# Two attention blocks merged on one core: values of merged sequences in bf16 high and low parts, and several small steps moved

## What is computed

```python
# block b: causal self-attention with 8 bit activations and ternary weights
q, k, v = bitlinear(x, Wq), bitlinear(x, Wk), bitlinear(x, Wv)   # 16 query heads, 4 key heads of 32
p = softmax(where(causal, -inf, rope(q) @ rope(k).T * scale))
x = layernorm(x + bitlinear(p @ v, Wo))
# block c: attention to 128 memory tokens, with a mask, a norm and a gate
n = rmsnorm(x, norm_w)
p = softmax(where(mask, (n @ wq.T) @ (ctx @ wk.T).T * scale, -inf))
x = layernorm(x + sigmoid(n @ wg.T) * ((p @ (ctx @ wv.T)) @ wo.T))
```

## Time and profile before

| | |
|---|---|
| Time, median of 3 runs | 3141.37 us (3140.55 to 3145.01) |
| The profiled execution's own time | 3140.32 us |
| Its span, from first to last instruction | 3138.5 us |
| PE busy over the span | 2855.3 us (91%) |
| DVE busy | 1852.7 us (59%) |
| ACT busy | 1584.2 us (50%) |
| POOL busy | 1214.4 us (39%) |
| Mean granted PE clock | 0.963 of full speed |

### The profile page before, as it was taken

One profiled execution on the slowest core, in us unless ns is written; L12 is line 12 of the kernel. 1 busy time (PEld: TensorE's weight loads), 2 busy tenths in 40 slices (PEclk: granted clock), 3 DMA queues, 4 the chain that ended last, 5 costly groups with the idle time before them and its releaser, 6 DMA issues. The chain is left out here.

```text
span 3138.5 us, 49654 instructions
## 1 busy us (share of the span) xinstructions
PE 2855.3 (91%) x17186; PEld 1677.1 (53%) x17186; DVE 1852.7 (59%) x3475; ACT 1584.2 (50%) x3632; POOL 1214.4 (39%) x1234
## 2 busy tenths in 40 slices
PE   6789887999999999689858999999679999999998
PEld 4676753555555555334336777766434444444443
DVE  5788977887787887587466666655522222222224
ACT  7999965655555555454157667665322122212211
POOL 4888967654454543144332111111411222122211
PEclk8999998999999999899969999999789999999999
DMA  4111113000000000310020000000100000000001
GB/s 157 51 44 45 45 45 104 28 8 4 7 7 4 7 4 1 124 38 1 15 103 18 15 14 17 15 18 15 64 1 31 31 32 1 31 32 31 1 1 54
DMA packets 35086, 99.01 MB, mean 32 GB/s; under 512 B 4933, under 2 KB 9413, under 8 KB 31686
## 3 DMA queue, kind: packets, MB, share of 16 engines
q1 hardware_dynamic: 34886, 96.46, 9.1%
HBM read 87.79 MB, written 4.46 MB: 29 GB/s over the span
## 5 line engine op out<-in xcount | busy, mean ns | idle before, releaser
L720 POOL TENSOR_TENSOR m_aTl<-m_prod,m_aTh 128x512 bf16<-128x512 f32 x96 | 111.1, 1157 | 675.4 <-ACT m_aTh L778 675.4
L945 DVE TENSOR_TENSOR m_prod<-m_bank,m_gated 128x512 f32<-128x512 f32 x96 | 66.4, 692 | 507.9 <-ACT m_gated L776 507.9
L1926 POOL TENSOR_TENSOR s_state<-s_state,s_ct 128x512 f32<-128x512 f32 x256 | 326.7, 1300 | 80.6 <-DVE s_state L2101 78.2
L2101 DVE TENSOR_TENSOR_SCAN s_state<-s_decay,s_psd 128x512 f32<-128x512 f32 x256 | 301.9, 1209 | 66.0 <-PE s_psd L2246 32.6
L776 ACT ACTIVATE m_gated<-m_bank 128x512 f32<-128x512 f32 x96 | 57.2, 596 | 550.2 <-PE m_bank L1037 550.2
L1035 PE MATMUL m_bank<-m_xTh,m_wh 128*128 128x512 bf16 x768 | 292.1, 380 | 0.0
L1036 PE MATMUL m_bank<-m_xTl,m_wh 128*128 128x512 bf16 x768 | 292.1, 380 | 0.0
L1037 PE MATMUL m_bank<-m_xTh,m_wl 128*128 128x512 bf16 x768 | 292.1, 380 | 0.0
L2246 PE MATMUL s_psd<-ident,s_v 128*128 128x128 f32 x1024 | 164.2, 285 | 42.8 <-DVE s_state L2101 22.3
L2002 ACT ACTIVATE s_decay<-s_dt,s_nega 128x508 f32<-128x508 f32 x256 | 181.8, 711 | 19.0 <-DVE s_state L2101 18.9
L2015 ACT ACTIVATE s_v<-s_uT,s_bT 128x512 f32<-128x512 f32 x256 | 182.3, 713 | 0.2
(11 more groups left out here) (491 smaller groups left out, 8029.0 us busy)
## 6 DMA issues: line engine op xcount, KB each, us to landing
m_stage<-in_moe_w_dram SPq DMA_DIRECT2D x8, 2352.0 KB, 9.4
s_ct<-ssm_bc SPq DMA_DIRECT2D x64, 256.0 KB, 3.1
X<-in_x_dram SPq DMA_DIRECT2D x4, 1024.0 KB, 11.1
a_cf<-in_ctxT_dram SPq DMA_DIRECT2D x16, 256.0 KB, 2.6
a_wstage<-in_xa_wq_dram SPq DMA_DIRECT2D x8, 512.0 KB, 3.9
a_wstage<-in_xa_wo_dram SPq DMA_DIRECT2D x8, 512.0 KB, 3.9
f_wstage<-in_ffn_wg_dram SPq DMA_DIRECT2D x4, 1024.0 KB, 7.2
f_wstage<-in_ffn_wu_dram SPq DMA_DIRECT2D x4, 1024.0 KB, 6.7
```

Source lines behind the costliest of these rows:

```text
L1926: pool.tensor_tensor(h, h, ct[t % 4][:, s * P:(s + 1) * P].unsqueeze(1).broadcast_to([P, KB, P]), ALU.mult).then_inc(weighted, 1)
L2101: dve.tensor_tensor_scan(state[i % RING][:, :], decay[t % 2][:, s, :, :].rearrange("p m t -> p (m t)"), ps_d[i % 2][:, :], 0.0, ALU.mult, ...
```

## The change

- For sequences that do not run alone, probabilities and values are kept as a bf16 high part and a bf16 low part, in the two halves of the old 32 bit tiles. ACT's copy writes the high part (high_part, to pTh); a new DVE step low_part subtracts it from b_pst and writes the low part (pTl). values then issues three products for each head where there was one. DVE also makes low parts of b's values (128 columns) and of c's values (512 columns), one of each in a turn. Sequences that run alone keep 32 bits.
- The wait that stood on the copy (copied) stands on the low part (low). So the other block's transposes wait for ACT's copy and for DVE's subtraction.
- turn_x moves on PE from the end of the steps of group 2 to group 3, behind turn_output, and from bank 0 to bank 2; copy_x on ACT follows; qx.scalar moves from group 1 to group 2, where it stands behind c's exponentials as before.
- c's memory values go through bank 0 in place of bank 2, so PE waits for mk_low (c_kT) before it computes them.
- On DVE: c's divide from group 0 to group 1, behind b's maxima; keys_low from group 1 to group 2; statistics of c's norm from group 3 to group 1, and its end from group 1 to group 2; qx.clip from 1 to 2; b_sc and b_osc are made earlier.

```diff
@@ class PairCore
+        self.vh = [v[:, :].bitcast(BF16)[:, 0:key_groups * P] for v in self.v]
+        self.vl = [v[:, :].bitcast(BF16)[:, key_groups * P:2 * key_groups * P] for v in self.v]
...
@@ def turn_probs(self, pe, s, g, other, turned_by_other):
-            pe.wait_ge(self.copied.sem, self.copied.at(s, g) if g else self.copied.at(s - 1))
+            pe.wait_ge(self.low.sem, self.low.at(s, g) if g else self.low.at(s - 1))
         if not isinstance(turned_by_other, int) or turned_by_other:
-            pe.wait_ge(other.copied.sem, turned_by_other)
+            pe.wait_ge(other.low.sem, turned_by_other)
...
@@ def values(self, pe, s, g, p):
-            mm = pe.matmul(out, self.pT[:, h, :], self.v[p][:, v:v + self.HW], start=True, stop=True)
+            if self.alone(s):
+                mm = pe.matmul(out, self.pT[:, h * P:(h + 1) * P], self.v[p][:, v:v + self.HW], start=True, stop=True)
+            else:
+                mm = three(pe, out, (self.pTh[:, h, :], self.pTl[:, h, :]),
+                           (self.vh[p][:, v:v + self.HW], self.vl[p][:, v:v + self.HW]), True, True)
         mm.then_inc(self.pv.sem, 1)
...
+    def low_part(self, dve, s, g):
+        if self.alone(s):
+            return
+        dve.wait_ge(self.high.sem, self.high.at(s, g + 1))
+        dve.tensor_tensor(self.pTl.rearrange("p h t -> p (h t)"), self.ps_t[:, :],
+                          self.pTh.rearrange("p h t -> p (h t)"), ALU.subtract).then_inc(self.low.sem, 1)
...
@@ scalar (ACT), turn
-                    if g == 1 and live(s + 2):
-                        qx.scalar(act, s + 2)
                     if g == 2:
+                        if live(s + 2):
+                            qx.scalar(act, s + 2)
...
@@ vector (DVE), new steps
+            def values(k, j):
+                if core.alone(k):
+                    return
+                dve.wait_ge(v_high.sem, v_high.at(k))
+                dve.scalar_tensor_tensor(core.vl[j], bank[2][:, NK:2 * NK], sc[j][:, 2:3], core.vh[j],
+                                         ALU.mult, ALU.subtract).then_inc(core.v_ready.sem, 1)
...
+            def memory_values(n, j):
+                if mcore.alone(n):
+                    return
+                dve.wait_ge(mv_high.sem, mv_high.at(n))
+                dve.scalar_tensor_tensor(mcore.vl[j], bank[0][:, :], mv[j][:, 0:1], mcore.vh[j],
+                                         ALU.mult, ALU.subtract).then_inc(mcore.v_ready.sem, 1)
...
@@ vector (DVE), turn
                     if g == 1:
-                        if live(m + 1):
-                            keys_low(m + 1)
+                        if live(m - 1):
+                            mcore.divide(dve, m - 1, o)
                         if live(s - 1):
                             output(s - 1)
-                        if live(s + 2):
-                            qx.clip(dve, s + 2)
                     if g == 2:
                         if live(s - 1):
                             qo.clip(dve, s - 1)
+                            output_scale(s - 1)
+                        if live(m + 1):
+                            keys_low(m + 1)
...
+                    if live(s):
+                        core.low_part(dve, s, g)
...
+                    if g == 2 and live(s + 2):
+                        qx.clip(dve, s + 2)
...
+                    if live(m):
+                        mcore.low_part(dve, m, g)
                     if g == 0:
                         if live(s - 1):
                             core.divide(dve, s - 1, o)
-                        if live(m - 1):
-                            mcore.divide(dve, m - 1, o)
...
+                    if g == 1 and live(m - 2):
+                        mln.statistics(dve, m - 2)
+                    if g == 2 and live(m - 2):
+                        mln.vector_end(dve, m - 2)
...
@@ tensor (PE)
             def turn_x(n):
                 pe.wait_ge(qx.steps.sem, qx.steps.at(n))
-                wait_of(pe, mk_low, n - LAG - 1)
-                edge(ln.steps, n - 4, 1)
-                out = bank[0][:, 0:256].bitcast(BF16)
+                wait_of(pe, core.k_ready, n - 1)
+                out = bank[2][:, 0:256].bitcast(BF16)
...
             def memory_values(n, j):
-                wait_of(pe, core.k_ready, n + LAG)
-                edge(mcore.q_ready, n)
+                pe.wait_ge(mk_low.sem, mk_low.at(n))
                 weights_split(n, 4)
-                product(bank[2][:, :], (cTh[j], cTl[j]), weights["v"], mproj)
+                product(bank[0][:, :], (cTh[j], cTl[j]), weights["v"], mproj)
...
-                    if g == 2:
-                        if live(s + 1):
-                            turn_query(s + 1)
-                            turn_key(s + 1)
+                    if g == 2 and live(s + 1):
+                        turn_query(s + 1)
+                        turn_key(s + 1)
+                    if g == 3:
+                        if live(s - 1):
+                            turn_output(s - 1)
                         if live(s + 2):
                             turn_x(s + 2)
-                    if g == 3 and live(s - 1):
-                        turn_output(s - 1)
```

More of the change, by code:

```diff
@@ L2402, in __init__ @@
         self.turned = Count(fr, f"{tag}_turned", 4)
-        self.copied = Count(fr, f"{tag}_copied", 4)
+        self.high = Count(fr, f"{tag}_high", 4)
+        self.low = Count(fr, f"{tag}_low", 4)
         self.pv = Count(fr, f"{tag}_pv", 4)
@@ L2445, in values @@
     def values(self, pe, s, g, p):
-        pe.wait_ge(self.copied.sem, self.copied.at(s, g + 1))
+        pe.wait_ge(self.low.sem, self.low.at(s, g + 1))
         if g == 0:
@@ L2478, in copy_part @@
             act.wait_ge(self.pv.sem, self.pv.at(s, g) if g else self.pv.at(s - 1))
-        act.activation(self.pT[:, :, :].rearrange("p h t -> p (h t)"), self.ps_t[:, :], ACT.Copy).then_inc(self.copied.sem, 1)
+        if self.alone(s):
+            act.activation(self.pT[:, :], self.ps_t[:, :], ACT.Copy).then_inc(self.low.sem, 1)
+            act.sem_inc(self.high.sem, 1)
+        else:
+            act.activation(self.pTh.rearrange("p h t -> p (h t)"), self.ps_t[:, :], ACT.Copy).then_inc(self.high.sem, 1)
     def maxima(self, dve, s, g):
@@ L2736, in copy_x @@
                 act.wait_ge(x_turned.sem, x_turned.at(n))
-                act.activation(xT[j][:, :, :].rearrange("p k t -> p (k t)"), bank[0][:, 0:256].bitcast(BF16), ACT.Copy).then_inc(xT_ready.sem, 1)
+                act.activation(xT[j][:, :, :].rearrange("p k t -> p (k t)"), bank[2][:, 0:256].bitcast(BF16), ACT.Copy).then_inc(xT_ready.sem, 1)
             def copy_output(n):
@@ L2744, in values @@
                 act.wait_ge(k_mul.sem, k_mul.at(n))
-                act.activation(core.v[j][:, :], bank[2][:, NK:2 * NK], ACT.Copy, scale=sc[j][:, 2:3]).then_inc(core.v_ready.sem, 1)
+                if core.alone(n):
+                    act.activation(core.v[j][:, :], bank[2][:, NK:2 * NK], ACT.Copy, scale=sc[j][:, 2:3]).then_inc(core.v_ready.sem, 1)
+                    act.sem_inc(v_high.sem, 1)
+                else:
+                    act.activation(core.vh[j], bank[2][:, NK:2 * NK], ACT.Copy, scale=sc[j][:, 2:3]).then_inc(v_high.sem, 1)
             def query_high(n, j):
@@ L2774, in memory_values @@
                 act.wait_ge(mcur_ready.sem, mcur_ready.at(n))
-                act.activation(mcore.v[j][:, :], bank[2][:, :], ACT.Copy, scale=mv[j][:, 0:1]).then_inc(mcore.v_ready.sem, 1)
+                if mcore.alone(n):
+                    act.activation(mcore.v[j][:, :], bank[0][:, :], ACT.Copy, scale=mv[j][:, 0:1]).then_inc(mcore.v_ready.sem, 1)
+                    act.sem_inc(mv_high.sem, 1)
+                else:
+                    act.activation(mcore.vh[j], bank[0][:, :], ACT.Copy, scale=mv[j][:, 0:1]).then_inc(mv_high.sem, 1)
             def keys_high(n):
@@ L2912, in output, with output_scale @@
                 qo.vector(dve, s, core.o[:, :], invo[:, :])
+            def output_scale(s):
+                dve.wait_ge(qo.steps.sem, qo.steps.at(s, 2))
+                if late(s, 1):
+                    dve.wait_ge(ln.steps.sem, ln.steps.at(s - 1, 1))
+                dve.tensor_scalar(osc[:, :], invo[:, :], sw[:, 3:4], None, ALU.mult).then_inc(oscaled.sem, 1)
             def end(s):
@@ L2964, in memory_end @@
                 dve.wait_ge(out_gated.sem, out_gated.at(s))
-                mln.vector(dve, s, gated[:, :], out_free.sem, 0.5)
+                dve.scalar_tensor_tensor(mln.r[:, :], gated[:, :], 0.5, fr.X[:, s, :], ALU.mult, ALU.add).then_inc(mln.steps.sem, 1)
             def turn(t, p):
@@ L3119, in branch @@
                 wait_of(pe, out_gated, s - LAG)
-                edge(mk_low, s + 2 - LAG)
-                edge(xT_ready, s + 3)
+                edge(mcore.v_ready, s + 2 - LAG)
+                edge(ln.steps, s - 1, 1)
                 for k in range(KB):
```

74 lines of the change are left out of this document (43 added, 31 removed).

## The result

Before 3143.89 us (median of 10 runs, 3138.32 to 3148.86), after 3153.69 us (10 runs, 3149.41 to 3158.27): a ratio of 1.0032, 95% interval 1.0023 to 1.0040. The change makes the kernel slower by 0.3%. The prediction said 3155 us. The total is right, but the working is not: two of its terms were wrong by about the same amount, in opposite directions, so that the number came out by luck.

The account below looks back on a forecast made before the run. PE's own length plus its waits bounds the merged turns: nine at +1.35 us (12.2), turn 14 about 1.0, turns 4 and 15 0.5 each, lone blocks 0; +14 on 3140.3 gives 3154, median 3155 us, range 3126 to 3171.

Parts of the forecast that it names:

- the three places: PE waits in a merged turn: 1.92 us at turn_memory_output (c_o), 1.33 at memory_values (c_kT), 1.75 at turn_x (b_q_int).
- the walk: One changed loop turn followed step by step through PE, ACT and DVE, giving 37.33 us in place of 35.98.
- the rule for a turn: Loop turn length: 35.98 + 1.35 + 6 (V - 0.50) us, as six of eight groups of values lie on PE's path.
- V: PE time of one group's values as 12 bf16 passes: 0.50 us taken, between 0.16 and 0.69, in place of 0.82.
- values of under 0.36 us: Sign that the prediction is wrong: one group's values on PE take less than 0.36 us.
- its rival in which gain and waits cancel: Passes so short that savings and PE's waits cancel: 3142 us, 3133 to 3147; chance 0.20.
- Turns with a block alone keep 32 bits: Turns where one block runs alone: moved steps fall inside existing waits, cost taken as 0, within 2 us.
- +14 from the merged turns: Turns 4 to 15, where both blocks run, together add 14 us.
- The second rival: DVE has c_o and c_kT ready in time, turn 34.4 us, near 3126 us in all; chance 0.16.
- The clock: PE's granted clock falling below 1.00 in the longer waits would make the kernel slower still; no size given.

Follow-up runs that it names:

- co_back: The changed kernel with only c's division (c_o) back in DVE's group 0, ahead of the low part of c's norm; 3139.1 us, ratio 0.9975.
- kt_back: The changed kernel with only the low part of c_kT (keys_low) back in group 1 on DVE; 3151.0 us, ratio 1.0016.
- x_back: The changed kernel with only the last two steps of the rounded x earlier (DVE group 1, head of ACT's group 2); 3146.4 us, ratio 1.0000.
- longer3: The changed kernel with three further low-by-low bf16 passes per head, 24 passes in place of 12 per group of values; 3183.3 us, ratio 1.0118.
- moves_only: The changed kernel with 32 bit values in every sequence, so all moves but no split and no low parts on DVE; 3196.2 us, ratio 1.0159.
- head_back: The changed kernel with x turned and copied at its old place, its last two steps in group 1, only in turns before 3; 3151.7 us, ratio 1.0020.
- three_head: all_three with x also turned and copied at its old place (group 2, bank 0) in the turns before 3; 3117.1 us, ratio 0.9916.
- tail_back: The changed kernel with c_o and c_kT at their old places only from turn 16 on; 3148.8 us, ratio 1.0009.
- all_three: The changed kernel with c_o, c_kT's low part and the last two steps of the rounded x at or near their old places; 3119.5 us, ratio 0.9918.

## Why the prediction was right, and where it was not

- *Right: the three places.* Waits of 1.27 + 0.22 + 0.26 = 1.75 us around c_o (1.92 forecast, small ones included), 1.23 for c_kT (1.33), 1.57 for b_q_int (1.75). co_back, kt_back and x_back each take one away, by the edit that the walk names as its cause.
- *Right near the measured values: the rule for a turn*, 35.98 + 1.35 + 6 (V - 0.50). At the measured V = 0.31 it gives 36.19, measured 36.05; at 0.60, 37.93, where longer3 has 37.7 to 38.1. At 0.82 it gives 39.25, and moves_only has 38.3 at full clock, 0.95 less: with the long values, and without the subtractions, the wait for c_kT is gone, which the rule has as a fixed part.
- *Mis-sized: V, the values of one group*, 0.50 us forecast and 0.31 measured. It was chosen "nearer the row with load and matmul in pairs", of 128 columns; with 32 columns the pair takes 26 ns, not 57.5. The Trainium skill (TensorE: Matmul & The Clock Gate, Back-to-back issue gap) gives about 25 ns for so few columns, and the trace agrees, with a new weight load ahead of each pass. The prediction had named values of under 0.36 us as a sign that it is wrong, and by this sign it was: what happened in the loop is its rival in which gain and waits cancel. By itself this size makes the merged turns come out at about +1.5 us in place of +14, and the sum at 3142, the "cancelled" rival. The ten intervals measured are 2.3 us shorter than before.
- *Wrong: "Turns with a block alone keep 32 bits; turn_x and the small steps move there inside waits that exist, so I take 0, within 2 us."* They cost 4.5 us at the head and 7.9 of the tail's 9.1. The step was argued from the idea that PE waits anyway in these turns. It does, but elsewhere, or for less: at the places of c_o and c_kT the kernel before waited 0.67 and 0.96 us in turn 16, and after 1.5 and 1.0 to 2.5, and in the head the moved copy of x puts the table load on the path. head_back and three_head bring back 2.7 and 2.4 us of the head's two steady intervals. tail_back brings back 3.9 of the tail's 7.9 us; the other 4.0 stay with the steps that it leaves moved, a lower clock in turn 16 among them, and which step it is stays open. I had read one turn of the loop in full, and no row of the tail.
- *So the mechanism was right for a loop turn, and the place of the loss was not; that the total fits is luck.* Forecast +14 from the merged turns and 0 from the ends; measured -2.3 and +13.6 in the profiled executions (turns 14 and 15, which the prediction counts as merged, lie in the tail here and make 1.2 of it), +9.8 between the medians. Of the 15.6 us between the profiled spans, 5.0 lie ahead of the first mark and are no effect of the change that I can show.
- *The second rival (DVE in time, 3126)* did not come true. all_three is nearly what it describes, and takes x's steps back as well: 3119.5.
- *The clock* was named as what would make it worse if the waits grew. In the loop of the kernel after it stays at 1.00; in turn 16 it falls to 0.94, where before had 1.00. In kt_back, where the wait for b_q_int is 2.0 us in place of 1.6, and in moves_only, where that for c_o is 1.6 in place of 1.3, it gives way in about every second turn of the loop, and in longer3 behind its two idle times of over 3 us.

## What to carry to other kernels

Price a move in every kind of turn that the program has, the first and last ones too: a step that pays for itself in the loop by work it saves has no such cover where the saving is switched off, and only a row from there shows what it waits for. Where a change consists of a saving and of moves, run the two apart: here the saving alone was worth 0.5%, the moves alone cost 1.6%, and the best kernel takes the saving and most of the moves, without the three that let a step which PE waits for come too late. And count overlapping passes by the pitch between their starts: a duration of 0.18 us says nothing of a cost of 0.026.

## What the runs showed of the hardware that I had not expected

- bf16 matmuls with 32 columns, each with its own 128x128 weight load, run at a pitch of 26 ns (12 in 0.31 us, 24 in 0.60 us).
- A little more waiting can cost much more than itself: in kt_back, in about every second turn, PE is granted 0.67 to 0.76 of full speed for some 6 us after a stretch with 1.71 of 3 us busy, which costs that turn 1.5 us. In the kernel after, where the wait for b_q_int is 1.6 us in place of 2.0, the clock stays at 1.00 in the loop, though it has a stretch with 1.57 of 3 us busy. I have not isolated what decides it.
- The same code took 20.7 us in one kernel and 24.3 in another: the third interval of the head, at a granted clock of 0.86 (after) and of 0.72 (tail_back), with 2.9 us more of PE busy.
- Two turns of longer3 have an idle time of 3.2 and 3.5 us on PE that is put down to "issue" and that no other kernel shows; what it is stays open.
